# A thirteenth table found by matmuls, grams in one piece, and gathers released by the ends of the grams

## The reference

```python
e = jnp.stack([tbl_0[ids[:, 0]], ..., tbl_26[ids[:, 26]]], axis=1)   # (512, 27, 128)
dot_products = jnp.einsum('bnd,bmd->bnm', e, e)
z = dot_products[:, c, r]                                            # 351 pairs, c, r = tril_indices(27, k=-1)
h = jnp.concatenate([z, dense_ctx], axis=1)                          # 351 + 16
h = jnp.maximum(h @ W_top1 + b_top1, 0.0)                            # 512 wide
h = jnp.maximum(h @ W_top2 + b_top2, 0.0)                            # 256 wide
y = h @ W_top3
```

## Time and profile before

| | us |
|---|---|
| median of three timed runs | 109.17 |
| span of the profiled execution (first to last instruction) | 123.6 |
| TensorE matmuls busy in it | 106.3 |
| VectorE busy | 70.0 |
| GpSimd busy, nearly all of it 62 gathers | 68.1 |
| ScalarE busy | 67.2 |

### The profile page before, as it was taken

How to read it: one execution, slowest core, us unless ns; L and a number is a source line. 1 busy time by engine, 2 the same in 40 slices (tenths; PEclk the granted TensorE clock), 3 DMA queues, 4 the chain that set the end, 5 groups by cost and what they waited for, 6 DMA issues and landing times.

```text
span 123.6 us, 3473 instructions
## 1 busy us (share of the span) xinstructions
PE 106.3 (86%) x1496; PEld 86.1 (70%) x1496; DVE 70.0 (57%) x98; ACT 67.2 (54%) x112; POOL 68.1 (55%) x71
## 2 busy tenths in 40 slices
PE   6998799899999899999329993789458999997992
PEld 6534487687887687788219883669448999797891
DVE  6799999999999999999900050015001060103401
ACT  4596929899999999995200052025301144531442
POOL 3777888888888888887744166416560665000000
PEclk9999999999999999999985599558975699999999
DMA  3896366966984574711210101110200011000000
GB/s 79 262 237 190 101 204 146 293 198 155 302 235 111 172 229 108 205 48 42 54 52 17 31 29 42 27 48 21 66 24 27 21 48 41 23 5 5 5 0 1
DMA packets 5305, 12.06 MB, mean 98 GB/s; under 512 B 1765, under 2 KB 2277, under 8 KB 5290
## 3 DMA queue, kind: packets, MB, share of 16 engines
q1 hardware_dynamic: 3282, 7.75, 22.0%
q0 software_dynamic: 1984, 4.07, 12.8%
q10 hardware_dynamic: 24, 0.02, 0.1%
HBM read 11.83 MB, written 0.00 MB: 96 GB/s over the span
## 4 chain that ended last, share of the span: by engine, by line
PE 68%; DVE 16%; issue 13%; ACT 1%; DVEq 0%
PE ring L512 21%; PE gram_ps L539 12%; DVE marks L651 10%; PE gram_ps L512 8%; PE ring L592 5%; PE ids_ps L574 4%; PE ring L523 4%; DVE low L628 3%; PE ids_ps L567 2%; PE ids_ps L523 2%; PE ring L574 2%; PE ring L602 2%; PE ids_ps L592 1%; DVE pick L610 1%; PE ids_ps L553 1%
## 5 line engine op out<-in xcount | busy, mean ns | idle before, releaser
L422 POOL DMA_INDIRECT rows<-tbl,ids_sb x62 | 67.1, 1082 | 36.3 <-issue 15.9
L651 DVE TENSOR_TENSOR marks<-ids_ps,row_no 125x1024 fp32r<-125x1024 f32 (+2 forms) x39 | 43.5, 1148 | 0.0
L512 PE MATMUL ring<-marks,high 125*128 125x512 f32 (+1 forms) x64 | 26.6, 416 | 1.7 <-issue 1.6
L539 PE MATMUL gram_ps<-rowsT 128*27 128x27 f32 x1024 | 15.8, 206 | 11.4 <-issue 11.2
L512 PE MATMUL ring<-marks,low 125*128 125x512 f32 (+1 forms) x64 | 25.2, 394 | 0.0
L539 PEld LDWEIGHTS gram_ps<-rowsT 128*27 128x27 f32 x1024 | 13.3, 118 | 14.7 <-issue 14.0
L512 PEld LDWEIGHTS ring<-marks,high 125*128 125x128 f32 x64 | 12.8, 200 | 7.1 <-issue 4.6
L724 ACT ACTIVATE away<-ids_ps,row_no 125x512 f32<-125x512 f32 (+1 forms) x22 | 14.0, 715 | 4.7 <-PE ids_ps L466 4.1
L628 DVE TENSOR_TENSOR low<-raw,high 125x512 fp32r<-125x512 f32 (+1 forms) x23 | 16.2, 705 | 0.0
L672 DVE STREAM_TRANSPOSE gram<-gram_ps 128x416 f32<-128x416 f32 (+1 forms) x8 | 4.6, 612 | 18.1 <-PE gram_ps L539 18.1
L512 PEld LDWEIGHTS ring<-marks,low 125*128 125x128 f32 x64 | 12.9, 202 | 1.6
(11 more groups left out here) (61 smaller groups left out, 116.5 us busy)
## 6 DMA issues: line engine op xcount, KB each, us to landing
raw<-tbl SPq DMA_DIRECT2D x9, 448.0 KB
raw<-tbl SPq DMA_DIRECT2D x2, 560.0 KB
rows<-tbl,ids_sb POOLq DMA_INDIRECT x62
w_sb<-w SPq DMA_DIRECT2D x2, 256.0 KB
w_sb<-w SPq DMA_DIRECT2D x1, 512.0 KB
raw<-tbl SPq DMA_DIRECT2D x9, 52.0 KB
raw<-tbl SPq DMA_DIRECT2D x2, 224.0 KB
w_sb<-w SPq DMA_DIRECT2D x1, 192.0 KB
```

The lines of the kernel that those rows point to most:

```text
L422: nc.gpsimd.indirect_dma_start(out=rows[0:n, i % ROW_BUFS, s, :], out_offset=None, in_=tables[PLACES[s]], in_offset=bass.IndirectOffsetOnA ...
L512: last = nc.tensor.matmul(bank[:, 0:n], part[:, i % SPLIT_BUFS, c * D:(c + 1) * D], mark_of(unit, c), start=c == 0 and part is high, stop= ...
L539: last = nc.tensor.matmul(gram_ps[s * STRIP:s * STRIP + F, g, 0:F], places, places, start=True, stop=True)
L651: nc.vector.tensor_tensor(marks_of(unit)[:, c0 - c1:, :], index.to_broadcast([TP, c1 - c0, n]), which.to_broadcast([TP, c1 - c0, n]), ALU. ...
```

## The change

One more table (6, 1250 rows) becomes a found one, for samples 256 to 511 alone: job 12, 256 columns, 10 chunks in three units of 4, 4 and 2 chunks. Tiles 2 and 3 have 14 gathers in place of 15, so there are 60 (0 to 16, 17 to 31, 32 to 45, 46 to 59). The four parts of each gram stand together in ORDER. The waits of PACE from gather 38 on are replaced by three: gather 38 waits for the end of gram 0, gather 42 for that of gram 1, gather 52 for that of gram 2.

```diff
 FOUND = [(1, 0, 8), (2, 0, 8), (8, 0, 8), (12, 0, 8), (15, 0, 8), (17, 0, 8), (18, 0, 8), (22, 0, 8), (23, 0,
-         8), (25, 0, 8), (0, 128, 10), (3, 128, 10)]
+         8), (25, 0, 8), (0, 128, 10), (3, 128, 10), (6, 256, 10)]
@@
-UNITS = [(j, c, c + chunks(n)) for j, (_, n) in enumerate(JOBS) for c in range(0, CHUNKS[j], chunks(n))]
+UNITS = [(j, c, min(c + chunks(n), CHUNKS[j])) for j, (_, n) in enumerate(JOBS) for c in range(0, CHUNKS[j], chunks(n))]
@@
-HALF = [units_of(j)[(len(units_of(j)) + 1) // 2][1] for j in range(len(JOBS))]
+HALF = [units_of(j)[min((len(units_of(j)) + 1) // 2, len(units_of(j)) - 2)][1] for j in range(len(JOBS))]
@@ ORDER
-find 10 1, gram 0 0, gram 0 1, find 11 0, gram 0 2, gram 0 3, find 11 1, turn 2 0, turn 2 1, gram 1 0
-gram 1 1, gram 1 2, pairs 0 0, pairs 0 1, turn 2 2, pairs 0 2, gram 1 3, turn 2 3, l1 0 0, l1 0 1
-l1 0 2, l1 0 3, l1 0 4, gram 2 0, gram 2 1, gram 2 2, pairs 1 0, turn 3 0, pairs 1 1, pairs 1 2
-l2 0 0, l2 0 1, gram 2 3, l3 0, l1 1 0, turn 3 1, l1 1 1, l1 1 2, l1 1 3, l1 1 4, l2 1 0, pairs 2 0
-l2 1 1, pairs 2 1, pairs 2 2, turn 3 2, l3 1, l1 2 0, turn 3 3, l1 2 1, gram 3 0, gram 3 1, l1 2 2
-l1 2 3, l1 2 4, gram 3 2, gram 3 3, l2 2 0, l2 2 1, pairs 3 0, pairs 3 1, l3 2, pairs 3 2, l1 3 0
-l1 3 1, l1 3 2, l1 3 3, l1 3 4, l2 3 0, l2 3 1, l3 3
+find 10 1, gram 0 0, gram 0 1, gram 0 2, gram 0 3, find 11 0, find 11 1, turn 2 0, pairs 0 0
+pairs 0 1, pairs 0 2, turn 2 1, gram 1 0, gram 1 1, gram 1 2, gram 1 3, find 12 0, find 12 1, l1 0 0
+l1 0 1, l1 0 2, l1 0 3, l1 0 4, pairs 1 0, pairs 1 1, pairs 1 2, turn 2 2, l2 0 0, l2 0 1, l1 1 0
+l1 1 1, l1 1 2, turn 2 3, l1 1 3, l1 1 4, l3 0, gram 2 0, gram 2 1, gram 2 2, gram 2 3, l2 1 0
+l2 1 1, turn 3 0, l3 1, pairs 2 0, pairs 2 1, pairs 2 2, l1 2 0, l1 2 1, l1 2 2, turn 3 1, l1 2 3
+l1 2 4, turn 3 2, turn 3 3, gram 3 0, gram 3 1, gram 3 2, gram 3 3, l2 2 0, l2 2 1, pairs 3 0
+pairs 3 1, pairs 3 2, l3 2, l1 3 0, l1 3 1, l1 3 2, l1 3 3, l1 3 4, l2 3 0, l2 3 1, l3 3
@@ PACE
-32 marks_used 30, 34 turned 6, 36 marks_used 35, 38 marks_used 38, 40 turned 9, 42 gram_part 2
-44 gram_part 3, 46 marks_used 50, 48 gram_part 5, 50 products 2, 52 l1_done 1, 54 gram_part 7, 56 paired 6
-58 products 3, 60 l1_done 7
+32 marks_used 30, 34 turned 6, 36 marks_used 35, 38 products 1, 42 products 2, 52 products 3
```

## The result

The kernel after takes 122.86 us in the median (122.44 to 123.38, four runs), before 109.19 us; the ratio is 1.125, 95% interval 1.121 to 1.129. The forecast was 115.8 us with a range of 111.5 to 119.0: the sign was right, the loss of 13.7 us is twice what was forecast. The profiled execution of after is one of the timed ones: it took 122.44 us with a span of 120.6 us, so 1.8 us lie outside the span (first to last instruction). The span of 123.6 us in the earlier trace rows was that of a disturbed execution; the runs of before that were timed beside e1 to e4 span 106.8 to 107.5 us at a clock of 1.0, which is again 1.8 to 1.9 us less than their times.

What follows compares the result with a forecast made beforehand. From gram 0 on, GpSimd's gathers were taken to bound the kernel. Replayed without stutter, before took 105.2 and after 112.3 us: 109.17 + 7.1 = 116.3, less 0.5 of stutter ended, 115.8 us; range 111.5 to 119.0.

Steps and rivals of the forecast that it cites:

- The sign and the waits: Forecast: slower (chance 0.83); gather 52's wait for gram 2 is dearest, leaving 5.4 us of TensorE bare before gram 3.
- G2: End of gram 2 on TensorE, forecast at 86.3 us; gather 52 was to wake 0.27 us after it.
- G1: End of gram 1 on TensorE, forecast at 72.1 us, against about 69.3 in the replay of before.
- The tail: Stretch from gram 3's end to the last instruction: 10.5 us, plus 0.5 for a clock that may be low.
- The prediction's own sign of being wrong: Forecast is wrong if grams still have holes with no gather under way, or if timed time falls with the span.
- Gram 0 in one piece hides nothing new: Gram 0 on TensorE: joining its parts costs nothing extra, as find 11 needs later marks anyway; priced at 2.5 us.
- Rival A: The stutter is real in timed runs and the change ends it, giving about 107.5 us; chance 0.14.
- the stutter: TensorE's idle holes in grams while gathers are under way; with low clock about 16 us, taken as nearly absent when timed.
- The remainder of 4.0 us: Timed median of before less its replayed 105.2 us: time outside the span and real stutter, 0.5 of it counted as ended.
- the replay: Sum of the kernel's stretches laid end to end without the stutter: 105.2 us before, 112.3 us after.
- VectorE's marks of table 6: Marks ahead of gram 0's regrouping on VectorE: 3.75 us, from 61.99 to 65.75, delaying pairs and gram 1.
- Gathers set the end of before: From gram 0 on GpSimd sets the end: gathers 1.25 us apart, gather 61 ending at 88.45 us.

Runs made afterwards that it cites:

- e1: The kernel before with each gram's four parts put together where the last part stood, nothing else; 117.07 us, ratio 1.069.
- e4: The kernel after with all of before's PACE waits in place of the three new ones; 119.26 us, ratio to before 1.083.
- e5: The kernel before, unchanged, profiled again for a trace of an execution whose time is that of the timed runs, 109.2 us.
- e6: The kernel after with 16 more idle matmuls (32 matmul records) on TensorE at its start; no time given.
- e12: The kernel before with grams 1 and 2 cut into pieces of 128 records, waits as before; 109.69 us, ratio 1.004.
- e8: The kernel after with VectorE's marks of table 6 behind gram 0's regrouping, not ahead of it; 123.19 us.
- e11: The kernel before without the PACE waits from gather 48 on, nothing else; 109.44 us, ratio 1.000.
- e14: The kernel before with the thirteenth found table alone (find 12 behind gram 1, 14 gathers in tiles 2 and 3); 112.15 us, ratio 1.013.
- e7: The kernel after with grams in two pieces, a step of slow instructions between them, and before's waits restored; 114.51 us, ratio 1.046.
- e9: e7 without find 12 (12 found tables, 62 gathers), gram 1 cut by the first two parts of l1 0; 111.31 us, ratio 1.021.

## Why the prediction was right and wrong

*The sign and the waits: right.* Gather 52 was woken 0.36 us after G2, the eight gathers took 9.7 us, and the stretch to gram 3 was 12.5 us (12.2 forecast). GpSimd waited 6.6 us for G1 (5 forecast), and TensorE stood 3.8 us for the last gathers and their copy, in five waits (4 to 6 forecast as a sign). The tail was 11.2 (11.0). The prediction's own sign of being wrong came true: grams have holes with no gather under way. The span fell only to 120.6 us, not to 112.5.

*"Gram 0 in one piece hides nothing new", and the same for grams 1 to 3: the step that failed.* It priced a gram in one piece at 2.5 to 3.3 us; it takes 4.9 to 5.8. I had read the price of 128 records from the earlier trace rows and doubled it. What made the doubling wrong is that one block of instructions can be run through in 1.3 us, and two can't. The slow steps between a gram's parts were that cover: find 11 between the halves of gram 0 gave the next block 2.3 us more (60.45 to 62.74 in e5). e1 puts this part at 7.5 to 7.9 us alone, e6 shows that it goes by the count of instructions, and the packets show the blocks arriving.

*Rival A named the fetch of instructions, but with the wrong conclusion.* It made gathers the cause and let the change cure it. Twelve packets were indeed too few for the stutter in the earlier trace rows; they are enough for the holes of after, one each. The rows of before could not give the price of a gram in one piece either: they hold no run of more than 128 records.

*The remainder of 4.0 us: mis-sized.* It was carried over to after nearly unchanged; there the profiled execution has 122.4 - 112.3 = 10.1 us. For before, 1.8 us lie outside the span, and the replay was 2.7 us shorter than e5: the last gather ended at 89.9 (88.45 in the replay), from there to gram 3 were 3.05 us (2.36), and gram 3 took 4.5 (3.9). None of these steps is shown to be a hole's doing, since e12 took the two long holes out without a gain. The remainder made before fit by construction, and it hid that the replay knew no holes.

*VectorE's marks of table 6, the main part of the 2.5 us for a later G1: wrong.* They came out at nothing (e8), because the hole in gram 0 and find 11 behind it lasted longer.

*Gathers set the end of before: wrong in part.* e11 removes waits without a gain, and e14 makes the kernel slower though it takes 2.5 us off GpSimd. In the page of e5 TensorE is busy for 92% of the span.

*Account of the 13.7 us*, in differences of medians: cuts and old waits restored, 8.35 (e7); table 6, 3.2 (e7 to e9); 2.1 are left to the rest of the order and are not told apart. The parts hold for this sequence of edits; by the ratios they are 8.6, 2.8 and 2.3.

*Rule and measurement.* The Trainium skill's gap of 6.2 us between a profile's total and the executed time ("Runtime: NRT & Kernel Launch", The ~15µs preamble/postamble breakdown) is about another quantity than the span of these pages: from the first to the last instruction the span is shorter than the time, by 1.8 us, and the 14.4 us of the earlier trace rows were an odd execution, not bookkeeping.

## What to carry to other kernels

Count a run of tiny matmuls in instructions, not only in time: here 192 to 256 matmul records with their weight loads in a row had a hole of 1.0 to 2.6 us where a second block ended within them (in gram 3 of e6 241 records passed first, as the block before had ended ahead of the gram). So put a step of 2 us of larger instructions between pieces of 128; the 8 matmuls of l2 in e7 were not enough. Before trusting a profile whose span is longer than the timed runs, ask which of its stalls can't be in them, and get the price of an uninterrupted run from a row that is as long as the one planned. A wait that keeps gathers out of a stretch moves their whole queue behind it; it paid 0.2 to 0.7 us per half gram here (1.54 to 1.96 us against 1.28 to 1.30) and cost 3.6 to 4.6.

## What the runs showed of the hardware that I had not expected

A block of instructions took 3.7 us from the start of the one before it until it ran (59.69 to 63.41), of which its packet is 1.4 us; in gram 1 it had the DMA queues to itself and still held TensorE up for 2.36 us. Where a hole falls is fixed by the count of instructions: 32 records more at the start moved three holes by exactly 32. Gathers under way slow a gram that has its instructions: 1.54 to 1.96 us for 128 records (e5) against 1.28 to 1.30. A hole can cost more than itself: behind that of gram 0 the granted clock was 0.52 from 64 to 67 us (1.2 GHz), and find 11 took 4.9 us for 20 matmuls, 3.5 at the full clock; behind that of gram 1 the clock stayed at 1.00.
